# Softmax row sums of the second layer: eight fp16 matmuls of a split running sum, behind the first projected tile

## The reference

```python
ht = (h @ W).reshape(N, N_HEADS, N_HIDDEN).transpose(1, 0, 2)
src = jnp.einsum('hnd,hd->hn', ht, a_src)
dst = jnp.einsum('hnd,hd->hn', ht, a_dst)
e = jax.nn.leaky_relu(src[:, :, None] + dst[:, None, :], SLOPE) + adj_mat[None]
att = jax.nn.softmax(e, axis=-1)
h_prime = jnp.einsum('hij,hjd->hid', att, ht)
return h_prime.mean(axis=0)
```

## Time and profile before

| | |
|---|---|
| median of 3 runs | 2618.03 us (2617.92 to 2619.28) |
| the profiled execution | 2618.63 us, of which the profile's span is 2616.7 us |
| TensorE (matmul records) busy | 2495.7 us, 95% |
| VectorE busy | 1953.4 us, 75% |
| ScalarE busy | 1246.3 us, 48% |
| GpSimd busy | 206.4 us, 8% |

### The profile page before, as it was taken

How to read it: one execution, slowest core, us unless ns; L and a number is a source line. 1 busy time by engine, 2 the same in 40 slices (tenths; PEclk the granted TensorE clock), 3 DMA queues, 4 the chain that set the end, 5 groups by cost and what they waited for, 6 DMA issues and landing times.

```text
span 2616.7 us, 46131 instructions
## 1 busy us (share of the span) xinstructions
PE 2495.7 (95%) x12326; PEld 1243.2 (48%) x12326; DVE 1953.4 (75%) x2856; ACT 1246.3 (48%) x1837; POOL 206.4 (8%) x206
## 2 busy tenths in 40 slices
PE   4899898859999999999999999999999999999997
PEld 1344346824444444444444444444444444444786
DVE  8998777558668766688666787677867777667774
ACT  5433344645445544455444554444544544444563
POOL 4104500300000000000000000000000000000000
PEclk8999998579999999999999999999999999999999
DMA  5443334420003000121001210022000210001000
GB/s 205 166 155 105 105 116 139 159 102 4 4 24 92 33 4 4 40 76 37 0 4 56 61 36 4 0 79 70 4 4 16 80 52 3 2 12 47 25 2 9
DMA packets 73560, 139.86 MB, mean 53 GB/s; under 512 B 4347, under 2 KB 11773, under 8 KB 72828
## 3 DMA queue, kind: packets, MB, share of 16 engines
q1 hardware_dynamic: 73468, 138.89, 16.5%
HBM read 125.17 MB, written 13.70 MB: 53 GB/s over the span
## 4 chain that ended last, share of the span: by engine, by line
PE 78%; issue 0%; DVE 0%; ACT 0%; POOLq 0%; POOL 0%
PE z_ps L1222 67%; PE o_ps L1246 10%; PE c_ps L1237 1%; DVE t_reg L1129 0%; ACT x_reg L1016 0%; DVE x_reg L1117 0%; DVE hl_reg L1095 0%; DVE ao_reg L1169 0%; DVE z_reg L1145 0%; ACT z_reg L1052 0%; POOLq L986 0%; POOL ticks L987 0%; POOLq L987 0%; POOLq L705 0%
## 5 line engine op out<-in xcount | busy, mean ns | idle before, releaser
L1222 PE MATMUL z_ps<-hl_reg,h_reg 128*128 (+2 forms) x8736 | 1759.7, 364 | 30.9 <-DVE hl_reg L1095 30.9
L1222 PEld LDWEIGHTS z_ps<-hl_reg,h_reg 128*128 (+1 forms) x8736 | 854.6, 98 | 932.6 <-DVE hl_reg L1095 31.3
L1040 ACT ACTIVATE hl_reg<-t_reg (+2 forms) x364 | 361.8, 994 | 734.2 <-DVE t_reg L1129 385.4
L1095 DVE TENSOR_TENSOR hl_reg<-t_reg,hl_reg (+2 forms) x364 | 417.6, 1147 | 229.7 <-ACT hl_reg L1040 223.6
L1025 ACT ACTIVATE t_reg<-ring_reg,vv 128x512 f32 (+3 forms) x728 | 526.4, 770 | 85.2 <-DVE ao_reg L1110 63.9
L1129 DVE SCALAR_TENSOR_TENSOR t_reg<-t_reg,vv,x_reg (+3 forms) x728 | 510.4, 743 | 13.7 <-issue 7.8
L1110 DVE TENSOR_TENSOR ao_reg<-ao_reg,t_reg 128x1024 f32<-128x1024 f32 (+1 forms) x336 | 383.8, 1142 | 0.0
L602 PE MATMUL z_ps<-t_reg,h_reg 128*128 (+2 forms) x1456 | 311.0, 375 | 52.1 <-DVE t_reg L384 45.7
L1246 PE MATMUL o_ps<-w_reg,z_reg 128*128 128x512 f16 x1248 | 273.9, 379 | 0.6 <-DVE z_reg L1145 0.6
L602 PEld LDWEIGHTS z_ps<-t_reg,h_reg 128*128 (+1 forms) x1456 | 144.8, 100 | 217.3 <-issue 62.8
L538 ACT ACTIVATE hl_reg<-t_reg 128x512 f16 (+3 forms) x182 | 107.6, 592 | 195.4 <-DVE t_reg L384 195.0
(11 more groups left out here) (106 smaller groups left out, 759.1 us busy)
## 6 DMA issues: line engine op xcount, KB each, us to landing
ring_reg<-adjT_in SPq DMA_DIRECT2D x78, 512.0 KB, 3.8
x_reg<-adjT_in SPq DMA_DIRECT2D x78, 512.0 KB, 3.7
t_reg<-x_in SPq DMA_DIRECT2D x13, 512.0 KB, 4.3
x_dram<-x_reg SPq DMA_DIRECT2D x13, 512.0 KB, 4.6
ring_reg<-rows_dram SPq DMA_DIRECT2D x24, 256.0 KB, 3.4
ao_reg<-x_dram SPq DMA_DIRECT2D x6, 1024.0 KB, 5.6
out_dram<-ao_reg SPq DMA_DIRECT2D x6, 1024.0 KB
w_reg<-W_in SPq DMA_DIRECT2D x5, 1024.0 KB, 8.1
```

What stands on the lines that cost most here:

```text
L1040: nc.scalar.activation(hl_ring[:, g % HL_RING, 0, :, 0:W], t_ring[:, g % T_RING, :, 0:W], ACT.Copy).then_inc(hi_ready, 1)
L1095: nc.vector.tensor_tensor(hl_ring[:, g % HL_RING, 1, :, 0:W], t_ring[:, g % T_RING, :, 0:W], hl_ring[:, g % HL_RING, 0, :, 0:W], ALU.subtr ...
L1222: mm = nc.tensor.matmul(z_ps[:, k, 0:W], hk[hs], hl_ring[:, r, ps, u, 0:W], start=first and u == 0 and n == 0, stop=last and u == 1 and n ...
```

## The change

The halves of `p_acc`, once added, are scaled by 2^-5 and split into two fp16 numbers, which lie in the place of the second half of `p_acc` (`acc16`). ScalarE makes the high one at the end of `evacuate`, VectorE the low one at the end of `evacuate_z`. The row sums are then fp16 matmuls, two for each 128 nodes, accumulated into the same column of `c_ps`, and are issued behind the first projected tile. `COEF` takes up the factor.

```diff
-COEF = 1.0 / (ZS * HS * WS * H)
+RS = 2.0 ** -5
+COEF = RS / (ZS * HS * WS * H)
...
+        acc16 = p_acc[:, :, 1].bitcast(F16).rearrange("p a (s i) -> p a s i", s=2)
...
                         nc.scalar.activation(z16[:, 0, k, 0:W], z_ps[:, k, 0:W], ACT.Copy,
                                              scale=ZS).then_inc(z_hi, 1)
+                    act.wait_ge(acc_sum, q + 1)
+                    nc.scalar.activation(acc16[:, h % 2, 0, 0:W], p_acc[:, h % 2, 0, 0:W], ACT.Copy,
+                                         scale=RS).then_inc(acc_hi, 1)
...
+                    dve.wait_ge(acc_hi, q + 1)
+                    nc.vector.scalar_tensor_tensor(out=acc16[:, h % 2, 1, 0:W], in0=p_acc[:, h % 2, 0, 0:W], scalar=RS,
+                                                   in1=acc16[:, h % 2, 0, 0:W], op0=ALU.mult,
+                                                   op1=ALU.subtract).then_inc(acc_lo, 1)
...
+                def row_sums(b, h):
+                    q = b * H + h
+                    pe.wait_ge(acc_lo, q + 1)
+                    pe.wait_ge(rs_sb, q + 1)
+                    for it in range(width(b) // P):
+                        for s in range(2):
+                            mm = nc.tensor.matmul(c_ps[:, it:it + 1], acc16[:, h % 2, s, it * P:(it + 1) * P],
+                                                  ones16[:], start=s == 0, stop=s == 1)
+                    mm.then_inc(rs_ps, 1)
+
                 def project(b, h):
...
-                    pe.wait_ge(acc_sum, q + 1)
-                    pe.wait_ge(rs_sb, q + 1)
-                    for it in range(n):
-                        mm = nc.tensor.matmul(c_ps[:, it:it + 1], p_acc[:, h % 2, 0, it * P:(it + 1) * P],
-                                              ones32[:], start=True, stop=True)
-                    mm.then_inc(rs_ps, 1)
                     pe.wait_ge(z_lo, (q + 1) * KT)
...
                         mm.then_inc(o_done, 1)
+                        if it == 0:
+                            row_sums(b, h)
```

More of the change, by code:

```diff
@@ L901, in gnn_kernel @@
         acc_sum = sem("acc_sum")
+        acc_hi = sem("acc_hi")
+        acc_lo = sem("acc_lo")
         rs_ps = sem("rs_ps")
```

## The result

The changed kernel has a median of 2601.95 us (2601.18 to 2603.49, 4 runs) against 2618.61 us for the kernel before in the same session: ratio 0.9937, interval 0.992 to 0.9954. Its profiled execution took 2603.49 us with a span of 2601.7. A second session gave 2603.94 us against 2617.81 (5 runs and 21), ratio 0.9947, interval 0.9933 to 0.996.

The account below looks back on a forecast made before the run. TensorE's nearly gapless stream was taken to bound the kernel. Savings of 14.6 us (wide segments) and 0.8 (256-wide), less 0.1 in the last, net 15.3: from the median of 2618.03 to 2602.7 us, range 2600.5 to 2608.5.

Parts of the forecast that it names:

- What bounds the kernel: Layer 1: TensorE alone stands in the chain until 2595.86 us, 78.51 us a segment; work added to other engines costs nothing.
- The fp32 sums go, the fp16 sums come: Row sums on TensorE: 0.81 us becomes 0.20 in 24 segments, 0.36 becomes 0.10 in three; net 15.3 us saved.
- The choice of 25 ns: Pace of each fp16 row-sum matmul, taken from four in layer 0; eight should take 0.20 us.
- (a): Row sums: the pace is slower than 25 ns; at 50 ns 10.1 us saved, 2607.9 us; chance 0.10.
- (b): Row sums: fp16 loads cost 97 ns or more, or accumulating matmuls wait 164 ns; 2617.5 us, no change; chance 0.08.
- The new operations: One more operation each on ScalarE (0.60 us) and VectorE (0.7) per segment, 36 us of work beside TensorE, costed at nothing.
- `rs_ps` later: VectorE behind the row sums: wait ahead of the reciprocal grows from 1.05 to about 2.4 us, costed at nothing.
- The thin place: VectorE at pair 10 of segment 24: thinnest cover in the trace, 0.9 us, expected to keep its lead.
- the cover of `acc_lo`: Projection behind tile 0: `acc_lo` posted near 1020.3, wanted at 1025.9; 5.5 us of cover, so no wait.
- rival (c): Mid-projection: TensorE waits for `acc_lo`, slower once it is 6.1 us later; 7 us gives 2643 us; chance 0.04.

Follow-up runs that it names:

- move alone: The kernel before with its fp32 row sums moved behind tile 0, nothing else changed: 2618.15 us, ratio 1.0003.
- four-times kernel: The changed kernel with each row-sum matmul issued four times into the same column, 32 in a row in place of 8: 2617.84 us, ratio 1.0 to the kernel before.

## Why the prediction was right

**What bounds the kernel.** It said that the kernel gets shorter by whatever TensorE's stream gets shorter by. Four kernels show it in the stretch: -15.25 (the change), +0.36 (move alone), +15.61 (24 more matmuls a segment on the changed kernel) and -2.60 us (four fewer), each what the matmuls by themselves come to. One reading was too wide: the granted clock isn't at nine tenths in the whole second layer, it is 0.50 from its start at 555.5 to 561 us, ahead of all that the change touches.

**The fp32 sums go, the fp16 sums come.** Sum of the prediction: 24 x 0.61 + 3 x 0.26 - 0.10 = 15.3 us. Measured: 0.61 in a wide segment; in a 256-wide one 39.60 less 39.34 us (the distance of two rows of the chain, 34.06 + 0.34 + 5.20 against 34.06 + 5.20 + 0.08), 0.26; and the end 0.10 longer (2586.72 - 2581.23 = 5.49 us against 2601.73 - 2596.34 = 5.39). To the nanosecond a wide segment gains 0.607 us (78.507 less 77.900 between the starts of two projections in the trace) and a 256-wide one 0.263, and 24 x 0.607 + 3 x 0.263 - 0.10 is 15.26, the stretch's 15.25. The predicted 2602.7 us lies between the medians of the two sessions; 2603.3 was forecast for the profiled execution, which took 2603.49.

The choice of 25 ns rested on four matmuls of layer 0. That eight in a row, each second one accumulating into the column just written, would go at that pace was open; the starts in the changed kernel show it, 25 ns apart after a first distance of 28, and the 32 in a row extend it. Rivals (a) and (b) had no support left after that. The Trainium skill's rule of a load as its columns divided by 1.2 per ns ("TensorE: Matmul & The Clock Gate", "LDWEIGHTS (loading the stationary operand)") would by estimate have made 32 loads 3.4 us; the trace has 0.80. For fp16 weights the measurement decides against it. With fp32 ones it is near: after a first distance of 0.03 us their records start 0.11 us apart in the trace of before, and the 0.10 of the prediction is the mean of both.

**The new operations.** Worked out at 0.60 and 0.7 us and costed at nothing: they measure 0.62 and 0.68, and alone they change the stretch by 0.00 us. The prediction had `acc_lo` 5.5 us ahead of its need; it is 5.4 us to the first load (5.65 to the first matmul).

**`rs_ps` later.** VectorE's wait ahead of the reciprocal was put at 2.4 us; it is 2.43, and tile 0's addition starts 1024.01 - 1020.47 = 3.54 us behind the end of the pairs, where before it started 1027.03 - 1023.27 = 3.76 us behind it: 0.2 us sooner, 0.3 worked out. The thin place that it named, pair 10 of segment 24, made TensorE wait in no trace.

**What it missed.** It took the cover of `acc_lo` as 5.5 us for every segment. Segment 23's is 2.9 us, since the pair that runs meanwhile is half as wide. That cost the change nothing, and showed only in the kernels with a later `acc_lo`.

The price of rival (c) was 2643 us for `acc_lo` 7 us later. The run had it 7.3 us later and took 2652; at 7.3 us the prediction's own sum has waits of 1.8 us and gives 24 x (1.8 - 0.61) + 3 x (1.8 - 0.26) + 0.1 = 33 us, 2651. That this is so near is luck, since its terms are off both ways. Too much stood for a wide segment, which loses 1.68 us, and for each of three 256-wide ones, which lose 0.83 (40.17 against 39.34). Too little stood for the last, which loses 2.3 where the sum has none, and for segment 23, which loses 5.83 (50.45 against 44.62): 4.2 us by its later start and 1.6 at the lower clock, of which the prediction had nothing.

**What isn't settled.** The medians of the two sessions differ by 2 us for the same kernel. In its two traces the difference lies ahead of the stretch; over the traces of all kernels here the first 336 matmuls ended between 626.1 and 631.1 us. Part of it is TensorE's clock. From 558 to 561 us the granted clock is 0.50 in the changed kernel's trace, where 9 matmuls fit in, and 1.00 in its repeat's, where 16 do. The first 336 matmuls take 75.41 us in the one and 74.00 in the other: 1.4 of the 2.0 us between the two executions. Of the 5 us by which the four-times kernel's trace is ahead, 2.9 are there already at the 365th matmul of layer 0 (130.7 us in place of 133.6). What moves these points from run to run stays open.

## What to carry to other kernels

When one engine's stream is gapless, price a change by its own instructions at the pace that the same kind of instruction keeps elsewhere in the trace (distance of starts, not record length), and read the other engines only for cover. Check the cover at the places where the loop changes its width or ends, not only in a typical round. And compare traces over a stretch that repeats: here it told differences of 0.3 us, where the medians scatter by two. Look at the granted clock before you name another cause for slow matmuls.

## What the runs showed of the hardware

- A matmul with 128x128 fp16 weights and one column costs 25 ns in a row of 4, 8 or 32, loads included, even when eight in succession add into the same column, though its load's record is 96 ns long and its own 163. An fp32 one stands as two loads and two matmuls and costs about 0.20 us with four in a row: eight times as much. Two fp16 halves of an fp32 operand therefore cost TensorE a quarter here, 0.20 us against 0.81 for 512 nodes (0.18 against 0.79 in the chain), and two operations on engines that had time to spare.
- Going from 512-column matmuls to one-column ones and back costs nothing in either place that was tried, ahead of tile 0 (0.18 us for the eight) and behind it (0.18).
- Layer 1's stretch repeats to 0.01 us: 1956.33 and 1956.34 us for the changed kernel in two sessions, 1971.58 for the kernel before and again for the one with two more operations beside TensorE. In these traces the scatter lies ahead of it.
- After 4.07 us without a matmul TensorE's granted clock fell from 1.00 to 0.50 (1.2 GHz), and up to 2467.67 us 512-column matmuls started 427 ns apart in place of 216. In the 23 segments of the same kernel with a wait of 1.51 us it stayed at 1.00.
